# A fused attention and feed-forward layer on eight cores: the bias addition of the first pass moved to VectorE, and the last 256 tokens reordered

## The reference

```python
x = layer_norm0(src)                                  # no gain, no bias
Q = elu(x @ Wq + bq) + 1;  K = elu(x @ Wk + bk) + 1;  v = x @ Wv + bv
KV = sum_s K v;  Z = 1 / (Q . sum_s K + 1e-6)         # 16 heads of 64
t  = layer_norm(x + (Q KV Z) @ Wo + bo, g1, be1)
u  = t + gelu(t @ W1 + b1) @ W2 + b2                  # W1: 1024 -> 4096, W2: 4096 -> 1024
xa = src + layer_norm(u, g2, be2)
out = xa + layer_norm0(xa) @ (weight.T + disha, folded over the 16 groups of 64)
```

## Time and profile before

| what | us |
|---|---|
| median of 3 runs | 1635.66 (1588.68 to 1702.76) |
| the profiled execution's own time | 1586.31 |
| its span, slowest core (core 7) | 1584.8 |
| spans of the eight cores | 1576.3 to 1584.8 |
| mean granted clock of TensorE, all cores | 0.985 to 0.989 |
| PE busy | 1514.8 |
| DVE busy | 985.3 |
| POOL busy | 497.2 |

### The profile page before, as it was taken

How to read it: one execution, slowest core, us unless ns; L and a number is a source line. 1 busy time by engine, 2 the same in 40 slices (tenths; PEclk the granted TensorE clock), 3 DMA queues, 4 the chain that set the end, 5 groups by cost and what they waited for, 6 DMA issues and landing times.

```text
span 1584.8 us, 27070 instructions; the slowest of 8 cores (1576.3 to 1584.8 us)
## 1 busy us (share of the span) xinstructions
PE 1514.8 (96%) x9428; PEld 902.3 (57%) x9428; DVE 985.3 (62%) x1042; ACT 542.8 (34%) x953; POOL 497.2 (31%) x438
## 2 busy tenths in 40 slices
PE   6799999999789999999999999999999999999995
PEld 2344445454356666666666666666666666666662
DVE  4567776666726675856667585765767576676314
ACT  2344445445533233232323233332323233232221
POOL 3545554454344313222221222222232222223101
PEclk9899999999889999999999999999999999999998
DMA  9977676548772223221222213121222322122111
GB/s 197 196 169 203 141 164 136 146 120 167 140 153 94 74 57 82 57 81 54 81 59 63 87 52 89 48 73 54 80 74 61 92 50 74 54 81 60 48 54 41
DMA packets 113428, 150.75 MB, mean 95 GB/s; under 512 B 67216, under 2 KB 75408, under 8 KB 113296
## 3 DMA queue, kind: packets, MB, share of 16 engines
q1 hardware_dynamic: 92656, 117.03, 25.4%
q0 software_dynamic: 14112, 25.70, 11.6%
q10 hardware_dynamic: 6528, 6.29, 1.5%
HBM read 117.53 MB, written 41.94 MB: 101 GB/s over the span
## 4 chain that ended last, share of the span: by engine, by line
PE 92%; DVE 2%; DMA 2%; issue 2%; ACT 1%; POOL 1%; DVEq 0%; ACTq 0%; POOLq 0%
PE psH L1290 28%; PE psY L1268 28%; PE psY L561 13%; PE psS L857 7%; PE psS L659 7%; PE psS L532 5%; DMA arena<-Wv 2%; PE psH L540 1%; PE psS L553 1%; PE psS L747 1%; DVE arena L458 1%; DVE arena L438 0%; PE psY L532 0%; ACT arena L355 0%; ACT arena L354 0%
## 5 line engine op out<-in xcount | busy, mean ns | idle before, releaser
L1290 PE MATMUL psH<-arena 128*128 128x256 bf16 x4096 | 531.9, 273 | 1.4 <-ACT arena L737 1.4
L1268 PE MATMUL psY<-arena 128*128 128x512 bf16 x2048 | 525.8, 379 | 0.4 <-DVE arena L780 0.4
L1196 ACT ACTIVATE arena<-psH,arena 128x256 bf16<-128x256 f32 x512 | 242.9, 474 | 766.5 <-PE psH L1290 764.6
L1290 PEld LDWEIGHTS psH<-arena 128*128 128x128 bf16 x4096 | 401.2, 98 | 145.4 <-issue 2.2
L1268 PEld LDWEIGHTS psY<-arena 128*128 128x128 bf16 x2048 | 200.3, 98 | 133.7 <-issue 1.6
L768 DVE RECIPROCAL arena<-arena 128x512 f32<-128x512 f32 x56 | 187.4, 3346 | 52.5 <-ACT arena L758 52.5
L561 PE MATMUL psY<-arena 128*128 128x512 bf16 x944 | 215.1, 382 | 0.7 <-DVE arena L469 0.7
L561 PEld LDWEIGHTS psY<-arena 128*128 128x128 bf16 x944 | 91.7, 99 | 106.7 <-issue 4.2
L708 POOL TENSOR_TENSOR arena<-arena 128x1024 f32<-128x1024 f32 x32 | 68.9, 2154 | 236.7 <-ACT arena L704 228.6
L654 POOL TENSOR_TENSOR arena<-arena 128x1024 f32<-128x1024 f32 x32 | 69.0, 2157 | 218.8 <-ACT arena L649 215.6
L668 DVE TENSOR_TENSOR arena<-psS,arena 128x512 f32<-128x512 f32 x60 | 41.3, 688 | 148.5 <-PE psS L659 148.5
(11 more groups left out here) (120 smaller groups left out, 1407.8 us busy)
## 6 DMA issues: line engine op xcount, KB each, us to landing
arena<-x SPq DMA_DIRECT2D x64, 512.0 KB, 4.8
arena<-W POOLq DMA_DIRECT2D x64, 256.0 KB, 7.8
xb_s<-arena SPq DMA_DIRECT2D x32, 512.0 KB, 5.6
arena<-xb_s SPq DMA_DIRECT2D x32, 512.0 KB, 3.2
out<-arena SPq DMA_DIRECT2D x32, 512.0 KB, 2.9
arena<-qt_s SPq DMA_DIRECT2D x16, 512.0 KB, 3.3
qt_s<-arena ACTq DMA_DIRECT2D x24, 256.0 KB, 7.8
arena<-WfT SPq DMA_DIRECT2D x16, 256.0 KB, 2.9
```

The costliest lines, as they stand in the source:

```text
L1196: sc.activation(hT[n % 3][:, :], hbank[n % 2], AF.Gelu, bias=b1c[:, c:c + 1]).then_inc(b_g, 1)
L1268: ii = te.matmul(ybank[k], hT[n % 3][:, (k // 2) * P:(k // 2 + 1) * P], w2_v[c][:, (k % 2) * HALF:(k % 2 + 1) * HALF], start=(c == 0), sto ...
L1290: ii = te.matmul(hbank[n % 2], w1_v[c // NCH][:, w, (c % NCH) * P:(c % NCH + 1) * P], x1T[i % 2][:, w, :], start=(w == 0), stop=(w == NCH ...
```

## The change

First pass. `x_be2` moves from POOL to DVE. Tiles 0 to 3 are added behind norm(5), tiles 4 and 5 at the end of iteration 4, tiles 6 and 7 at the end of iteration 5, and tile t + 2 in each iteration t from 6 on, between stats(t+3) and the second q_out. Only tiles 0 to 7 have buffers of their own; from tile 8 on the two buffers of the ring are used, the sum is written to the staging tile `xbst`, and the load of tile t + 2 waits for the addition of tile t. stats(6) and norm(6) now stand ahead of k_in(4), and ACT's rstd(6) ahead of k_exp(4). On SP, be2 is loaded right after tiles 4 and 5, ahead of the wait for Wv, and tile 7 ahead of three small constants; stores of tiles 0 and 1 and loads of tiles 8 and 9 follow at once. POOL waits for K tile 3 before its first k_sum, does the four first k_sums together and then the four first weight loads.

End. In i = 15, from chunk 8 on (EARLY = 32 - 24), the gelu results are kept in 24 buffers `hL`, and the second product is made for sub 0 only. Sub 1's 48 matmuls for these chunks are made after the last chunk. DVE does all of sub 0's work up to the centred tile, then all of sub 1's. The norm is split: `centre` subtracts the mean only, by column halves; PE transposes and ACT copies out each half; the 16 matmuls go by the halves of the inner dimension; and the reciprocal root is multiplied in at the end, in `scaled`, which replaces `o_add`. Sub 1 has its own bf16 tiles (`nbL[1]`, `nTL[1]`), and the results go to four banks of their own. Its output is stored in two halves, by SP and by ACT.

```diff
@@ sync_a
             sy.wait_ge(s_wk[NCH - 1], 16)
             x_load(4)
             x_load(5)
+            sy.dma_start(be2b[:, :], be2_d).then_inc(s_be2, 16)
             sy.wait_ge(s_wv[NCH - 1], 16)
             x_load(6)
-            for dst, src in [(be2b, be2_d), (onesb, one_d), (b1c, b1_d), (bvc, bvc_d)]:
+            x_load(7)
+            for dst, src in [(onesb, one_d), (b1c, b1_d), (bvc, bvc_d)]:
                 sy.dma_start(dst[:, :], src).then_inc(s_rows, 16)
-            x_load(7)
-            for t in range(T):
+            x_keep(0)
+            x_keep(1)
+            x_load(8)
+            x_load(9)
+            for t in range(2, T):
                 x_keep(t)
-                if t < 10:
-                    x_load(t + 8)
-                elif 16 <= t < T - 2:
+                if 8 <= t < T - 2:
                     x_load(t + 2)
@@ x_load
-                if t >= 18:
+                if t >= 10:
                     sy.wait_ge(a_xb, t - 1)
                     sy.wait_ge(a_src, t - 1)
                 elif t >= 8:
-                    sy.wait_ge(s_xo[t % 8], 16 if t < 16 else 32)
+                    sy.wait_ge(s_x01[t - 8], 16)
@@ pool_a
-            gp.wait_ge(a_src, 6)
+            gp.wait_ge(a_kb, 4)
             for t in range(4):
                 k_sum(t)
+            for t in range(4):
                 w_load(t)
             for t in range(4, T):
-                for u in (XB[t] if t < 16 else [t + 2] if t + 2 < T else []):
-                    x_be2(u)
                 k_sum(t)
                 w_load(t)
@@ dve_a
+            def x_be2(t):
+                if t == 0:
+                    v.wait_ge(s_be2, 16)
+                if t >= 9:
+                    v.wait_ge(s_xbst, 16 * (t - 8))
+                elif t < 8:
+                    v.wait_ge(a_src, t + 1)
+                v.tensor_tensor(xbst[:, :] if t >= 8 else x_buf(t)[:, :], x_buf(t)[:, :],
+                                be2b[:, :], ALU.add).then_inc(a_xb, 1)
...
             norm(5)
+            for t in range(4):
+                x_be2(t)
+            stats(6)
+            norm(6)
             for t in range(4, T):
                 if 5 <= t < T - 2:
                     norm(t + 2)
                 k_in(t)
                 k_out(t)
-                if t == 4:
-                    stats(6)
-                    norm(6)
                 if t < T - 4:
                     q_out(v, 2 * (t - 4))
                 if t + 3 < T:
                     stats(t + 3)
+                if 6 <= t < T - 2:
+                    x_be2(t + 2)
                 if t < T - 4:
                     q_out(v, 2 * (t - 4) + 1)
+                if t in (4, 5):
+                    x_be2(2 * t - 4)
+                    x_be2(2 * t - 3)
@@ y_step
-            for k in range(4):
+            for k in range(2 if n >= NFCH * LAST + EARLY else 4):
@@ the end: DVE
+            for sub in range(2):
+                sums(sub)
+                u_gain(v, LAST, sub)
+                xa(v, LAST, sub)
+                centre(sub)
+            for sub in range(2):
+                scaled(sub)
...
+                v.scalar_tensor_tensor(half, eF[sub][nh], rx[sub][:, 0:1], half, ALU.mult,
+                                       ALU.add).then_inc(b_o, 1)
@@ the end: PE
             y_step(te, NFCH * NSUP - 1)
+            for k in (2, 3):
+                for c in range(EARLY, NFCH):
+                    ii = te.matmul(ybank[k], hL[c - EARLY][:, P:2 * P],
+                                   w2_v[c][:, (k % 2) * HALF:(k % 2 + 1) * HALF], start=False,
+                                   stop=(c == NFCH - 1))
+                ii.then_inc(b_yd, 1)
+            for sub in range(2):
+                for nh in range(2):
+                    te.wait_ge(e_cen, 2 * sub + nh + 1)
...
+                    for c in range(4):
+                        ii = te.transpose(sbf[nh][:, c * P:(c + 1) * P],
+                                          nbL[sub][:, nh * HALF + c * P:nh * HALF + (c + 1) * P],
+                                          identb[:, :])
+                    ii.then_inc(e_tn, 1)
...
+                for nc4 in range(2):
+                    te.wait_ge(e_nT, 2 * sub + nc4 + 1)
+                    for nh in range(2):
+                        for c in range(4 * nc4, 4 * nc4 + 4):
+                            ii = te.matmul(eF[sub][nh], nTL[sub][:, c, :],
+                                           wf_v[:, c, nh * HALF:(nh + 1) * HALF],
+                                           start=(c == 0), stop=(c == NCH - 1))
+                        if nc4 == 1:
+                            ii.then_inc(b_wf, 1)
```

More of the change, by code:

```diff
@@ L116, in build_nc @@
         ksb = VB(W + 59392, D).rearrange("p (c s) -> p c s", c=NCH)
+        hL = [VB(b + 512 * k, 256) for b in (W + 45056, W + 51200, W + 57344) for k in range(8)]
+        nbL = [nb, b2b]
+        nTL = [nT, chunks(VB(W + 24576, D))]
         o = W + 61440
@@ L159, in build_nc @@
         s_x = [sema("x_in%d" % k) for k in range(8)]
-        s_xo = [sema("x_out%d" % k) for k in range(8)]
+        s_x01, s_xeo, s_be2 = [sema("x0_out"), sema("x1_out")], sema("xe_out"), sema("be2_in")
         s_xbst = sema("xb_out")
@@ L321, in w_load @@
                 if t == 16:
-                    for k in range(8):
-                        gp.wait_ge(s_xo[k], 32)
+                    gp.wait_ge(s_xeo, 96)
                 if t < NFCH - 1:
@@ L827, in n_norm @@
             v.wait_ge(b_rx, n)
-            if sub == 1 and j == NSUP - 1:
-                v.wait_ge(b_tn, 1)
-            elif sub == 1:
+            if sub == 1:
                 v.wait_ge(s_tn[0], 16 * (j + 1))
@@ L834, in n_norm @@
             else:
[L835 removed]
+                v.wait_ge(s_tx[1], 16 * j)
             v.tensor_scalar(nb[:, :], home(j, sub)[:, :], mvx[sub][:, 0:1], rx[sub][:, 0:1],
                             ALU.subtract, ALU.mult).then_inc(b_n, 1)
[L839 to L849 removed]
         def final(te, j, sub, nh, bank):
[L852 to L855 removed]
+            te.wait_ge(s_tn[sub], 16 * (j + 1))
             for c in range(NCH):
@@ L1179, in pool_b, with h_buf @@
                 bo_add(gp, i + 2, 0)
+        LAST = NSUP - 1
+        EARLY = NFCH - len(hL)
+        def h_buf(n):
+            c = n - NFCH * LAST
+            return hL[c - EARLY] if c >= EARLY else hT[n % 3]
         def y_done(n):
@@ new lines, in act_e, with sums, centre, scaled @@
+            sc.wait_ge(b_o, 4 * LAST + 4)
+            sc.dma_start(out_d[(T - 1) * P:T * P, HALF:D], home(LAST, 1)[:, HALF:D]
+                         ).then_inc(s_oe, 16)
+        def dve_e(v):
+            def sums(sub):
+                n, hm = 2 * LAST + sub + 1, home(LAST, sub)
+                for nh in range(2):
+                    u_add(v, LAST, 2 * sub + nh)
+                    v.wait_ge(b_u, 4 * LAST + 2 * sub + nh + 1)
+                    ii = v.bn_stats(bnst[2 + sub][:, nh, :], hm[:, nh * HALF:(nh + 1) * HALF])
+                ii.then_inc(b_bnu, 1)
+                v.wait_ge(b_bnu, n)
+                v.bn_aggr(mvu[sub][:, :], bnst[2 + sub][:, :, :]).then_inc(b_mvu, 1)
+            def centre(sub):
+                v.wait_ge(b_mvx, 2 * LAST + sub + 1)
+                if sub == 0:
+                    v.wait_ge(s_tn[1], 16 * LAST)
+                for nh in range(2):
+                    v.tensor_scalar(nbL[sub][:, nh * HALF:(nh + 1) * HALF],
+                                    home(LAST, sub)[:, nh * HALF:(nh + 1) * HALF],
+                                    mvx[sub][:, 0:1], None, ALU.subtract).then_inc(e_cen, 1)
+            def scaled(sub):
+                for nh in range(2):
+                    half = home(LAST, sub)[:, nh * HALF:(nh + 1) * HALF]
+                    v.wait_ge(b_wf, 4 * LAST + 2 * sub + nh + 1)
+                    if nh == 0:
+                        v.wait_ge(b_rx, 2 * LAST + sub + 1)
+                    v.scalar_tensor_tensor(half, eF[sub][nh], rx[sub][:, 0:1], half, ALU.mult,
[5 more added lines that the diff above has]
+                centre(sub)
+            for sub in range(2):
+                scaled(sub)
```

108 lines of the change are left out of this document (38 added, 70 removed).

## The result

| | before | after |
|---|---|---|
| profiled execution, us | 1586.31 | 1564.08 |
| span of core 7 in it, us | 1584.8 | 1562.5 |
| median of its runs in the comparison, us | 1612.17 (4 runs, 1584.02 to 1702.76) | 1564.65 (4 runs, 1563.18 to 1791.87) |

The ratio after to before is 0.9862, 95% interval 0.9834 to 0.989: 1.4% faster. Profiled execution against profiled execution, 22.2 us are gone; 25 were forecast.

What follows compares the result with a forecast made beforehand. PE, busy 96% of the span, was taken to bound the kernel, leaving only its idle or lower-clock places to gain. 1586.3 - 14 (first pass) - 11 (end) = 1561 us; own range 1553 to 1572, range given 1550 to 1612.

Steps and rivals of the forecast that it cites:

- The first pass: Moving x_be2 to DVE and the new order gain 6 + 9 - 1 = 14 us; bounds 3 and 19.
- The hole: At 66 us PE waits 6.92 us for norm(6), then runs at lower clock; gain 6 us, bounds 2 and 10.
- The small holes: Between iterations 6 and 18, second q_out held by POOL's x_be2 pairs makes PE wait; 9 us gained.
- The ring of two buffers: First pass: load(t+2) now waits for x_be2(t), so source tiles may come late; cost 1 us, bounds 0 and 8.
- eight heavy iterations: First-pass iterations with two weight loads, where x's landing of 8 us runs a few tenths over.
- The limit of 7.9 us: First pass: issue, landing, statistics and addition fit into 11.25 us if x's landing takes under 7.9.
- The end: After the last second product: sub 0's chain hidden behind 48 matmuls, sub 1's shortened; gain 11 us, bounds 8 and 14.
- stage f's stall: Behind 3.38 us of idle PE in stage f, 11 matmuls took 3.73 us, part at the lower clock.
- 1: Rival: only one part pays, either first pass gains 5 or the end stays at lower clock; 1572 us, chance 0.16.
- 3: Rival: x lands late, near 12 us, in every heavy iteration and the kernel is slower; 1589 us, chance 0.05.
- 4: Rival: k_sum and x_be2 hold each other, q_out stays late; 1569 us, chance 0.12.
- 2: Rival: be2 costs Wv nothing, end matmuls keep higher clock, other cores gain like core 7; 1553 us, chance 0.12.

Runs made afterwards that it cites:

- a1: The kernel before with only the first-pass part of the change: 1572.54 us, ratio 0.9917 to the kernel before.
- a3: The kernel before with only tile 6's statistics, norm and root moved ahead of iteration 4, x_be2 left on POOL: ratio 1.0044 to the kernel before.
- c1: The changed kernel with stores of tiles 2 to 7 behind later loads and 16 filling matmuls at the end: 1558.5 us, ratio 0.9813 to the kernel before.
- c2: The changed kernel with be2's load moved back behind the wait for Wv and tile 6's load: 1563.11 us in one run.
- b1: The changed kernel with unread additions on POOL, two per iteration in 5 to 15, one in 16 to 27: 1578.6 us in one run.
- b2: The changed kernel with the xb stores of tiles 2 to 7 issued one by one behind the loads of tiles 10 to 15: lowest run 1558.97 us.
- a2: The kernel before with only the end part of the change (reordered last 256 tokens): 1577.12 us in one run.
- b4: The changed kernel with 12 instead of 24 chunks of sub 1's second product held back: span 1565.5 us on core 3.
- b3: The changed kernel with 16 unread matmuls on PE between sub 0's last matmul and sub 1's transposes: lowest run 1558.11 us.

## Why the prediction was right or wrong

**The time.** The step that failed is the one that set the sum beside the runs: "1586.3 - 14 - 11 = 1561" is in the time of the profiled execution, and I gave it as the time beside a median of 1635.66, which it undercuts by 4.6%, where the sum itself says 1.6% and the runs 1.4%. I had seen the 3.1% between them and left both in the text (1561 and "near 1610"). What the runs showed in its place: the kernel before takes 1584.05 to 1587.0 beside a1 to a3 and 1584.5 to 1587.22 beside c1, so 1586.3 is its own time, the 3.1% belong to the draw of three runs, and the sum stands without them. In its own time the forecast was 25 us, the measurement 22.2, and 1564.65 lies in its own range, 1553 to 1572.

**The first pass: 14 forecast, 13.3 on core 7, 14 for the part alone (a1), median of the cores 11.2.** The terms, on core 7:
- The hole, forecast 6: iteration 6 began 8.7 us earlier. I had charged be2 with 2.7 us on Wv and DVE's order with 1; Wv's last chunk cost PE 1.1 us (the V product's 16 matmuls start at 46.09 instead of 44.98), and the query product ahead of the hole began as much later, at 65.53 instead of 64.42; of the second charge nothing is to be seen. Core 7 is the mildest of the eight in the first charge, which is 1.1 to 3.6 us by core between before and after; c2 puts it at 1.5 to 2 by the medians, nearer to the 2.7 than core 7 shows. On core 7 the hole was also nearly at its deepest: iteration 6 of before began at 80.9 to 87.2 by core, and of after at 77.9 to 79.4, 2.3 to 9.0 us earlier, 6.5 in the middle. That and the late tile below spread the cores' gains from 8.5 to 15.0.
- The small holes, forecast 9: gone, 9.2 us on core 7; q_out takes 0.69. b1 and a3 show that POOL's pairs of additions made them.
- The ring of two buffers, forecast a cost of 1: this is the term that was mis-sized, 4.6 us on core 7, 1.4 to 6.8 by core. I looked for it in eight heavy iterations at 0.1 us each, and it was one landing, 13.67 us against the 8 expected, where the stores of six tiles stand in front. The prediction counted the store that gates a load, not the six that the new loop order issues from 68 us on. b2 shows this by taking them away. DVE's wait for x was to stay below 10 us in all; it was 12.5 on core 7, more than half of it for tile 10. The limit of 7.9 us agrees with b2, where nothing is lost at 7.8, but isn't tested by it: a single landing of 8.9 us on the same core (tile 12) cost PE nothing either.
- So 13.3 beside 14 is in part luck on core 7: the hole gave 2.7 us more than forecast, and the ring took 3.6 more. By the middle of the cores the hole was as forecast, and the ring makes nearly all of the difference.
- The addition on DVE, 1.2 taken: 1.20, and 1.65 where k_sum was running, the 0.4 us of the prediction. With that, the rule of the Trainium skill, "SBUF — State Buffer", section "Who interferes with whom", held in the form the prediction gave it: held in turn, and inside the slack. The 5.47 us of before and the 8.14 of a3 go further than one instruction's length: DVE's instruction was held for two of POOL's, and for three.

**The end: 11 forecast, 11.3 on core 7, 10.7 in the middle of the cores, 9.4 to 10.5 for the part alone (a2).** 18.4 us from the last second product, 17 to 20 forecast. The gap of 0.29 at the last chunk was forecast as 0.3. Sub 0's chain is hidden (b4: of 5.2 us of cover taken away 2.7 to 4.6 come back). PE's idle stretch ahead of sub 1's transposes was 3.75 us, against 3, and the 16 matmuls behind it took 5.30 (5.1 to 6.1 by core), against 5.5, a choice that rested on stage f's stall; b3 shows that the idle stretch is the cause, at 1.7 us on core 7.

**What the sum lacked.** Stage f and the main part gave back 2.3 us on core 7, and gave or took up to 2.4 on the others. In the main part PE waits 1.27 us once, at 480.92, for a gelu, and the timelines of after show what stood ahead of it.

```profile
475.96 0.22 POOL L686 TENSOR_SCALAR arena<-arena 128x1 f32<-128x1 f32 x1
477.00 2.21 DVE L698 SCALAR_TENSOR_TENSOR arena<-arena 128x1024 f32<-128x1024 f32 x1 [6.14 <-POOL arena L689]
479.35 1.06 ACT L710 ACTIVATE arena<-arena 128x1024 bf16<-128x1024 f32 x1 [2.77 <-DVE arena L698]
480.31 0.46 ACT L1198 ACTIVATE arena<-psH,arena 128x256 bf16<-128x256 f32 x1
480.92 1.02 PE L1270 MATMUL psY<-arena 128*128 128x512 bf16 x4 [1.27 <-ACT arena L1198]
```

The gelu is behind ACT's copy (L710), the copy waits for DVE (L698), DVE for a small root on POOL, and the root stands in POOL's stream behind additions that wait for loads of WfT: it starts 7.3 us after its statistics, in before 5.0 us. That is read from the timelines; no run tests it.

**The rivals.** 1 had the right mechanism in part (a late tile, but one and not eight) at under half of its price (4.6 us where it had 10); in the time of the profile it gave 1572, 8 us too much. 3 is excluded: one landing was over 12 us, not eight. 4 is excluded by q_out at 0.69 throughout. 2 was wrong in two of its three parts: be2 cost Wv some 2 us where it had none, and the matmuls of the end didn't keep the higher clock.

## What to carry to other kernels

An instruction of one engine that takes several times its usual duration, with another engine's pair of operations beside it, is a price of the other engine's work: moving that work can cost the receiving engine less busy time than it frees, here 38 us of additions against some 52 us (38 + 14, an estimate from the busy times of the two kernels) of being held. When a buffer ring is shortened, look for what is issued ahead of its first load, not only at the mean landing: stores that nobody waits for can make the one load late that everybody waits for. Take a forecast's percentage from the profiled execution's own time, and distrust a median that stands well above the fastest run.

## What was unexpected

- A 512 KB load behind six 512 KB stores, issued over the 23 us ahead of it, took 13.67 us to land (12.2 to 14.6 by core), the stores themselves 14.5 to 21.3; with the stores spread the same load took 7.8 (7.5 to 10.4).
- Two POOL additions back to back held DVE for both (5.47 us in the earlier trace rows, 4.32 in a3) or for only one (2.52 in b1); in a3 one DVE instruction was held through three of POOL's, 8.14 us.
- 16 matmuls that nobody reads, put into 3.75 us of waiting, shortened the end by 1.2 to 2.7 us by core: the 16 real ones behind them took 3.61 us instead of 5.30, since the granted clock did not fall (b3).
